# A gated MLP whose rows are normalised, scaled and split in row layout, and turned by DMA transposes instead of TensorE

## The reference

```python
h = shift_token(x)                       # columns 128..255 come from the row before
mu = h.mean(-1, keepdims=True)
var = h.var(-1, keepdims=True)
h = (h - mu) / jnp.sqrt(var + 1e-05) * lg + lb
h = h @ w1 + b1                          # 256 x 1364
a, g = jnp.split(h, 2, axis=-1)          # HID = 682 each
h = a * jax.nn.gelu(g, approximate=False)
x = x + h @ w2 + b2                      # 682 x 256
```

## Time and profile before

| | |
|---|---|
| median of three runs | 4297.88 us |
| profiled execution, its own time | 4296.06 us |
| its span | 4294.4 us |
| granted TensorE clock, mean over the span | 0.951 |
| busy over the span: TensorE, VectorE, ScalarE, GpSimd | 3835.2, 3330.0, 2558.9, 1191.1 us |

### The profile page before, as it was taken

One profiled execution on the slowest core, in us unless ns is written; L12 is line 12 of the kernel. 1 busy time (PEld: TensorE's weight loads), 2 busy tenths in 40 slices (PEclk: granted clock), 3 DMA queues, 4 the chain that ended last, 5 costly groups with the idle time before them and its releaser, 6 DMA issues. The chain is left out here.

```text
span 4294.4 us, 94790 instructions
## 1 busy us (share of the span) xinstructions
PE 3835.2 (89%) x38292; PEld 2167.2 (50%) x38292; DVE 3330.0 (78%) x5467; ACT 2558.9 (60%) x3449; POOL 1191.1 (28%) x966
## 2 busy tenths in 40 slices
PE   7999999769998969998986999999999999866996
PEld 4788888535655535555553332332333333334664
DVE  5688988779985569985687889999998978584444
ACT  3566666646553435653443777787888887744553
POOL 1022321267761067771141000000000000033552
PEclk9999999889999989999997999999999999977998
DMA  1010100133330033430072000000000000034664
GB/s 63 5 40 28 43 25 25 41 70 64 63 51 28 0 63 66 65 55 9 0 160 47 9 9 2 9 2 2 9 2 2 9 2 9 4 100 93 117 134 111
DMA packets 325878, 175.39 MB, mean 41 GB/s; under 512 B 239508, under 2 KB 316520, under 8 KB 324968
## 3 DMA queue, kind: packets, MB, share of 16 engines
q1 hardware_dynamic: 302856, 133.88, 14.8%
q0 software_dynamic: 13440, 21.24, 2.9%
q10 hardware_dynamic: 9184, 14.68, 1.4%
HBM read 77.81 MB, written 38.58 MB: 27 GB/s over the span
## 5 line engine op out<-in xcount | busy, mean ns | idle before, releaser
L2257 DVE TENSOR_REDUCE s_tops<-ps 128x2 f32<-128x1024 f32 (+3 forms) x1152 | 1252.2, 1132 | 143.2 <-PE ps L2143 103.6
L2226 ACT ACTIVATE s_weights<-ps 128x1024 f32<-128x1024 f32 (+3 forms) x1152 | 1092.5, 952 | 344.3 <-PE ps L2156 193.8
L2178 PE MATMUL ps<-s_weights,v_flat 128*32 128x256 f32 (+1 forms) x8704 | 692.1, 390 | 7.4 <-ACT s_o_t L2232 6.1
L2137 PE MATMUL ps<-keys,s_q 48*128 48x512 f16 (+3 forms) x2304 | 435.0, 375 | 46.0 <-DVE s_tops L2257 26.0
L2156 PE MATMUL ps<-s_q,keys 50*128 50x512 f16 (+3 forms) x2304 | 434.0, 374 | 46.9 <-DVE s_tops L2257 33.3
L2293 POOL CAST s_shift<-s_minus_top 128x16 f16<-128x16 f32 x32 | 6.3, 196 | 1429.9 <-DVE s_minus_top L2264 1429.9
L583 PE MATMUL ps<-a_qt,a_kt 128*128 128x256 f16 x3072 | 375.3, 273 | 3.8 <-POOL s_ones L538 3.8
L2156 PEld LDWEIGHTS ps<-s_q,keys 50*128 50x128 f16 x2304 | 112.2, 93 | 512.3 <-issue 246.7
L1174 PE MATMUL ps<-attention_w,la_yt 128*128 128x512 f16 x1152 | 289.3, 399 | 37.8 <-DMA la_yt<-la_y_parts 30.3
L583 PEld LDWEIGHTS ps<-a_qt,a_kt 128*128 128x128 f16 x3072 | 300.9, 98 | 40.3 <-POOL s_ones L538 4.2
L1249 ACT ACTIVATE la_weights<-ps 128x1024 f32<-128x1024 f32 x124 | 126.8, 1023 | 291.5 <-PE ps L1164 291.5
(11 more groups left out here) (372 smaller groups left out, 7158.0 us busy)
## 6 DMA issues: line engine op xcount, KB each, us to landing
ex_whole<-in_L_ffn_w_dram ACTq DMA_DIRECT2D x14, 1024.0 KB, 10.2
qk_parts<-a_parts SPq DMA_DIRECT2D x64, 128.0 KB, 4.3
keys<-qk_parts SPq DMA_DIRECT2D x48, 128.0 KB, 5.7
s_q<-qk_parts SPq DMA_DIRECT2D x48, 128.0 KB, 5.0
x<-in_x_dram SPq DMA_DIRECT2D x8, 512.0 KB, 9.3
attention_w<-attention_split SPq DMA_DIRECT2D x2, 2048.0 KB, 9.1
la_table<-in_rotary_dram SPq DMA_DIRECT2D x64, 64.0 KB, 2.1
a_table<-in_rope_dram POOLq DMA_DIRECT2D x8, 512.0 KB, 6.1
```

The source lines that it names most:

```text
L2137: mm = pe.matmul(m.ps[:, bank, 0:width], b.q[rows(half, KEY_PARTS * L1_DH), place % 2, pair, t * P:(t + 1) * P], m.keys[rows(half, KEY_PAR ...
L2178: mm = pe.matmul(m.ps[h * QUAD:(h + 1) * QUAD, OUT, begin:end], m.v_flat[:, first:first + QUAD], weights[:, a % 2, h, begin:end], start=(k ...
L2226: act.activation(weights[:, a % 2, 2 * pair:2 * pair + 2, skip:CHUNK], m.ps[:, bank:end + 1, skip:CHUNK], ACT.Exp).then_inc(s["exp"], 1)
L2257: dve.tensor_reduce(tops[:, u % 2, :, i % 2, t, c], m.ps[:, bank:end + 1, 0:width], AX.X, ALU.max).then_inc(s["max"], 1)
```

## The change

The rows stay in row layout until they are split. `norm` is as before, one count for each tile of rows. GpSimd multiplies by `ln_g` and adds `ln_b` (`gain`), which now have to be there as rows spread over all partitions, and two DMAs load them so. ScalarE rounds a chunk's high part (`high`), VectorE makes the low part (`parts_low`), and SP issues four DMA transposes that write `ht`. The shift by one row is not copied any more, apart from one column that GpSimd copies at a chunk's edge (`edge`): for the second half of the columns TensorE reads `ht` one column early (`EDGE - k`). PSUM banks 0 and 1 are free, and "up" has three pairs (`RING`) instead of two; two tiles of the next chunk (`AHEAD`) stand before down instead of one. Chunk 0 is made tile by tile by VectorE and ScalarE.

```diff
-    TURN_AT = ET - 4
-    NORMED_BY = {1: 0, 2: 1, 4: 2, 5: 3}
+    RING, AHEAD = 3, 2
+    EDGE = 16
+    HIGH_AT, LOW_AT = 0, 1
+    NORMED_BY = {0: 0, 1: 1, 2: 2, 3: 3}
...
-        ht_whole = sb("ht_whole", [P, 2, KD, CHUNK + 4])
-        ht = sb("ht", [P, 2, 2, KD, CHUNK], F16)
+        parts = sb("parts", [P, 2, TPC, 2, D], F16)
+        ht = sb("ht", [P, 2, 2, KD, EDGE + CHUNK], F16)
+        before = sb("before", [P, 1])
+        lng_row, lnb_row = sb("lng_row", [P, D]), sb("lnb_row", [P, D])
...
+                for to, name in ((lng_row, "ln_g"), (lnb_row, "ln_b")):
+                    sp.dma_start(to[:, :], layer_of(a[name], layer).rearrange("o d -> (o d)").partition_broadcast(P)).then_inc(s["rows_in"], 16)
...
+                def turn(c):
+                    if c:
+                        need(sp, s["low"], c)
+                        need(sp, s["ht"], 16 * TPC * c)
+                        need(sp, s["a_mm"], ET * (c - 1))
+                    for j in range(TPC):
+                        at = EDGE + j * P
+                        if c == 0:
+                            sp.wait_ge(s["first_low"], j + 1)
+                        sp.dma_start_transpose(ht[:, c % 2, :, :, at:at + P].rearrange("p a k t -> p (a k) t"),
+                                               parts[:, c % 2, j, :, :].rearrange("p a d -> p (a d)")).then_inc(s["ht"], 16)
+                turn(0)
                 move_down(sp, m, s, 1)
                 if not last:
                     load_attention(sp, m, a, layer + 1, s["next_in"])
                 move_up(sp, m, s, 1)
+                for c in range(1, CHUNKS):
+                    turn(c)
...
+                def edge(c, u):
+                    need(pool, s["ht"], 16 * TPC * (c + 1))
+                    need(pool, s["a_mm"], ET * c)
+                    pool.tensor_copy(ht[:, 1 - u, :, 1, EDGE - 1:EDGE], ht[:, u, :, 1, EDGE + CHUNK - 1:EDGE + CHUNK]).then_inc(s["edge"], 1)
+
+                def gain(c, u):
+                    for j in range(TPC):
+                        whole = normed[:, u, j, :]
+                        need(pool, s["normed"], TPC * (c - 1) + j + 1)
+                        pool.tensor_tensor(whole, whole, lng_row[:, :], ALU.mult).then_inc(s["gained"], 1)
+                        pool.wait_ge(s["gained"], TPC * (c - 1) + j + 1)
+                        pool.tensor_tensor(whole, whole, lnb_row[:, :], ALU.add).then_inc(s["whole"], 1)
+
+                def step(c, u):
+                    bias(c, u)
+                    if exists(c + 1):
+                        edge(c, u)
+                    if exists(c + 2):
+                        gain(c + 2, u)
+
+                pool.wait_ge(s["rows_in"], 32)
+                gain(1, 1)
                 rows_on_gpsimd(pool, m, s, 1)
-                in_pairs(pool, CHUNKS, bias)
+                for c in range(CHUNKS):
+                    step(c, c % 2)
...
-                    need(dve, s["turned"], KD * (c - 1))
+                    need(dve, s["low"], c - 2)
...
-                def ht_low(c, u):
-                    need(dve, s["a_mm"], ET * (c - 1))
-                    for k in range(KD):
-                        need(dve, s["ht_high"], KD * c + k + 1)
-                        dve.tensor_tensor(ht[:, u, 1, k, :], ht_whole[:, u, k, 0:CHUNK], ht[:, u, 0, k, :], ALU.subtract).then_inc(s["ht"], 1)
+                def parts_low(c, u):
+                    need(dve, s["high"], c)
+                    dve.scalar_tensor_tensor(parts[:, u, :, 1, :], normed[:, u, :, :], 1.0, parts[:, u, :, 0, :], ALU.mult, ALU.subtract).then_inc(s["low"], 1)
+                def whole_of_first(j):
+                    parts_of_row = [(slice(0, P), m.own), (slice(P, D), m.next)]
+                    for h, by in parts_of_row:
+                        n = dve.scalar_tensor_tensor(normed[:, 0, j, h], m.y[:, j, h], by[:, 0, j:j + 1], lng_row[:, h], ALU.subtract, ALU.mult)
+                    n.then_inc(s["first_gained"], 1)
+                    dve.wait_ge(s["first_gained"], j + 1)
+                    for h, by in parts_of_row:
+                        n = dve.scalar_tensor_tensor(normed[:, 0, j, h], normed[:, 0, j, h], by[:, 1, j:j + 1], lnb_row[:, h], ALU.mult, ALU.add)
+                    n.then_inc(s["first_whole"], 1)
+
+                def low_of_first(j):
+                    dve.wait_ge(s["first_high"], j + 1)
+                    dve.scalar_tensor_tensor(parts[:, 0, j, 1, :], normed[:, 0, j, :], 1.0, parts[:, 0, j, 0, :], ALU.mult, ALU.subtract).then_inc(s["first_low"], 1)
...
                 def gate(c, u, between=None):
-                    if exists(c + 2):
-                        dve.wait_ge(s["back"], 32)
...
-                        if e == TURN_AT + 1 and exists(c + 1):
-                            ht_low(c + 1, 1 - u)
-                        elif e and e <= TPC + 1 and exists(c + 2):
+                        if e == LOW_AT and exists(c + 1):
+                            parts_low(c + 1, 1 - u)
+                        if e in NORMED_BY and exists(c + 2):
                             norm(c + 2, u, range(NORMED_BY[e], NORMED_BY[e] + 1))
...
                     low(ET - 1)
+                    if exists(c + 2):
+                        dve.wait_ge(s["back"], 32)
...
-                norm(0, 0)
+                dve.wait_ge(s["rows_in"], 32)
+                for j in range(TPC):
+                    whole_of_first(j)
+                    if j:
+                        low_of_first(j - 1)
+                low_of_first(TPC - 1)
                 half_rows_on_vector(dve, m, s, 1)
+                dve.wait_ge(s["edge_high"], 1)
+                dve.tensor_tensor(ht[:, 0, 1, 1, EDGE - 1:EDGE], before[:, :], ht[:, 0, 0, 1, EDGE - 1:EDGE], ALU.subtract).then_inc(s["edge_low"], 1)
                 norm(1, 1)
-                ht_low(0, 0)
                 rows_on_vector(dve, m, s, 1)
                 dve.wait_ge(s["zeroed"], 1)
...
-                def scaled(c, u):
-                    need(act, s["ht"], KD * (c - 1))
-                    need(act, s["turned"], KD * c + 1)
-                    act.activation(ht_whole[:, u, 0, 0:CHUNK], m.ps[:, 0, :], ACT.Identity, bias=b.lnb[:, 0:1], scale=b.lng[:, 0:1]).then_inc(s["ht_whole"], 1)
-                    need(act, s["turned"], KD * c + 2)
-                    need(act, s["ht_whole"], KD * c)
-                    act.copy(ht_whole[:, u, 1, 0:1], ht_whole[:, 1 - u, 1, CHUNK:CHUNK + 1])
-                    act.activation(ht_whole[:, u, 1, 1:CHUNK + 1], m.ps[:, 1, :], ACT.Identity, bias=b.lnb[:, 1:2], scale=b.lng[:, 1:2]).then_inc(s["ht_whole"], 1)
-                    need(act, s["a_mm"], ET * (c - 1))
-                    for k in range(KD):
-                        need(act, s["ht_whole"], KD * c + k + 1)
-                        act.copy(ht[:, u, 0, k, :], ht_whole[:, u, k, 0:CHUNK]).then_inc(s["ht_high"], 1)
+                act.copy(ht[:, 0, 0, 1, EDGE - 1:EDGE], before[:, :]).then_inc(s["edge_high"], 1)
+
+                def high_of_first(j):
+                    act.wait_ge(s["first_whole"], j + 1)
+                    act.copy(parts[:, 0, j, 0, :], normed[:, 0, j, :]).then_inc(s["first_high"], 1)
+
+                def high(c, u):
+                    act.wait_ge(s["whole"], TPC * c)
+                    need(act, s["ht"], 16 * TPC * (c - 1))
+                    act.copy(parts[:, u, :, 0, :], normed[:, u, :, :]).then_inc(s["high"], 1)
...
-                            high(e - 1)
-                        if e == TURN_AT and exists(c + 1):
-                            scaled(c + 1, 1 - u)
-                    high(ET - 1)
-
-                scaled(0, 0)
+                            hid_high(e - 1)
+                        if e == HIGH_AT and exists(c + 1):
+                            high(c + 1, 1 - u)
+                    hid_high(ET - 1)
+
+                for j in range(TPC):
+                    high_of_first(j)
                 act.wait_ge(s["zeroed"], 1)
                 run(gelus, act.Fori)
...
-                def turn(c, u):
-                    need(pe, s["normed"], c + 1)
-                    for k in range(KD):
-                        need(pe, s["ht_whole"], KD * (c - 1) + k + 1)
-                        for j in range(TPC):
-                            t = pe.transpose(m.ps[:, k, j * P:(j + 1) * P], normed[:, u, j, k * P:(k + 1) * P], m.ident[:, :])
-                        t.then_inc(s["turned"], 1)
...
-                    need(pe, s["ht"], KD * (c + 1))
+                    need(pe, s["ht"], 16 * TPC * (c + 1))
+                    if isinstance(c, int) and c == 0:
+                        pe.wait_ge(s["edge_low"], 1)
+                    else:
+                        need(pe, s["edge"], c)
...
                         for part, mm_sem, free in ((1, s["g_mm"], s["gelu"]), (0, s["a_mm"], s["hid_whole"])):
-                            need(pe, free, ET * c + e - 2 + 1)
+                            need(pe, free, ET * c + e - RING + 1)
```

(42 more changed lines are left out.)

16 lines of the change are left out of this document (8 added, 8 removed).

## The result

The changed kernel takes 4317.02 us (median of 6 runs, 4310.10 to 4331.99), beside 4296.26 for the kernel before in the same rounds: a ratio of 1.005, interval 1.0039 to 1.0062; the medians lie 20.8 us apart. The forecast was 4311. The profiled execution took 4312.28, 16.2 more than that of before (4296.06), which is the comparison that the traces explain.

The account below looks back on a forecast made before the run. TensorE was taken as the bound, busy 114.66 of 118.2 us. Steady part +3.5, start +5, output stage -1.5 and clock +6 sum to +13; added to the median 4297.88 this gives 4311 us, range 4279 to 4333.

Parts of the forecast that it names:

- The saving, 1.95 a chunk: TensorE's steady MLP chunk: turn and wait for the last hid go, leaving 21.79 us if nothing else is late.
- What is late next: Tiles ahead wait 2.1 us for parts_low and four transposes after down; period 23.9 against 23.74, steady part +3.5.
- The collisions: GpSimd's gain beside VectorE's low(0) and parts_low at a chunk's start: 0 to 1.3 us, taken as 0.4.
- The start: Start of each MLP: first up 4.9 us later at 1316.6, first down's end +2.4 a layer, +5 for both.
- turn(1) not late: MLP start: the +5 leaves out a late turn(1), which appears only in the upper bound of +12.
- The end of a stage, no term: Each MLP's end unchanged: a 2.99 us wait for hid, then down takes 10.48 instead of 7.43.
- The output stage, -1.5: Output stage: take_h ahead of high cuts TensorE's wait by up to 1.04 at about two places; -1.5.
- The clock, +6 for 2 of 12: Two of twelve stalls at the tiles ahead drop TensorE's clock, 3.05 us for a slow down: +6, possible 0 to 37.
- D: Rival: up's reads shifted one element run at half pace, adding about 115 us: 4413; chance 0.03.
- C: Rival: transposes overlap, all four land by D + 9.1 (D: down's end), TensorE never stalls: period 21.79, 4278; chance 0.22.
- E: Rival: every stall at the tiles ahead costs clock, +37 in place of +6: 4342; chance 0.05.
- rival B: An even exchange: stalls cost no clock and collisions cancel, +2: 4300; chance 0.29.

Follow-up runs that it names:

- low_in_down: The changed kernel with parts_low(c+2) at the start of residual(c), beside down(c), a whole down earlier: 4294.99 us, ratio 0.9993.
- all_three: low_in_down with the rows of gain and shift loaded in the stage before and GpSimd's bias behind down's third tile: 4282.39 us, ratio 0.9960.
- swap_alone: The kernel before with only the output stage's swap, ScalarE's take_h ahead of high: 4299.00 us, ratio 1.0004.
- ahead_1: all_three with one tile of the next chunk ahead of down instead of two, three buffers kept: 4292.22 us, ratio 0.9986.
- one_piece: The changed kernel, but chunk 0's four transposes all wait until the last piece's low part is made: 4329.23 us, ratio 1.0072.
- low_at_2: The changed kernel with parts_low one tile later in gate, behind low(1): 4375.69 us, ratio 1.0178.

## Why the prediction was right, point by point

- **The saving, 1.95 a chunk: right.** 21.79 was forecast for a chunk with nothing late; low_in_down and all_three have 21.92, a saving of 1.82.
- **What is late next: right, in place and size.** L1554 started 3.08 behind down's end (3.00), the first tile ahead at 11.41 (11.3), the wait was 2.05 (2.1), the chunk 24.03 (23.9). From the first down's end to the seventh's layer 1 grew by 1.0 us (forecast 1) and layer 0 by 5.5, 1.7 of it clock (2.5 and clock): layer 0's waits were 2.3 to 2.8. One bound was summed wrongly: with the first tile ahead at 12.9 a chunk is 25.5 us, not 25.0, and the upper bound of the steady part +21, not +15.
- **The collisions: named, and undersized.** 0.64 instead of 0.4. Missed was the one that matters once the stall is gone: `bias`, in the new order behind `gain`, now starts just ahead of the gate's last two subtractions and stretches them from 1.46 to 3.44 or 5.54. And a `norm` (one tensor operand from SBUF) was not priced: it takes 0.75 beside `gain` instead of 0.34.
- **The start: the first up right (1316.27, forecast 1316.6), what follows undersized.** +2.4 a layer was forecast; less the tile more that is done by then (2.59), the first down ended 3.4 us later in layer 0 and 6.0 in layer 1. "turn(1) not late" failed: waits of 1.12 and 1.45. And the comparison was read from layer 0 alone, whose first chunk took 29.05 us from first matmul to down's end; layer 1's took 27.83. The same two chunks took 30.21 and 28.18 in swap_alone, so 1.5 of the 9.4 for both layers is within what an unchanged MLP differs by.
- **The end of a stage, no term: wrong for layer 1, and luck for layer 0.** Layer 0 got 2.9 us back because the clock stayed up, but so it did in swap_alone with the MLP of before; the prediction took the 10.48 of one execution for fixed. Layer 1 gave back 2.3 of the 2.59 that it should have saved, 1.1 of it wait: with a tile more done beforehand, VectorE's last gate with `add_to_x` has less under it, and the wait is 4.09 (4.49 in all_three, and 2.99 in ahead_1, which has one tile ahead). The other 1.2 is clock.
- **The output stage, -1.5: not borne out.** The wait moved to VectorE.
- **The clock, +6 for 2 of 12: too high in this execution, and priced too high.** One wait (2.31) was followed by slow matmuls, and they cost 1.7, not 3.05. In one_piece three of eleven such waits were, so the share of 2 in 12 is not refuted. That after's runs lie up to 19.7 above the profiled one could be more such drops; no trace of a slower run was taken, so it stays open.
- **The rivals.** D fell: the mean of the "up" matmuls is 380 ns with the shifted reads and 379 before. C is what happens once `parts_low` starts a chunk's down earlier; as the code stands it failed where the prediction said, at four landings by D + 9.1. E came true only for the longer waits of low_at_2.

Of the sum of +13, the MLPs had 14.5: steady part 3.5, start 5, clock 6. Measured were 15.0: about 4.8, 9.4 and 1.7, with -0.9 at the ends. So the mechanism (one longer wait, on the chain from down's end to the fourth transpose, for the turn and the old wait) was right, but that the total came so close is luck: two terms are wrong by 4 us each way, and layer 0's end gave 2.9 by its clock. The medians lie 6 us further up than this sum, and the range was wide enough to hold rival B too, so the rows and not the total show that the prediction was right.

## What to carry to other kernels

Work taken off the bounding engine is worth what the new chain's latency leaves: add up from the event that starts it (here the end of down, since VectorE's order put `parts_low` behind it) to the moment its result is wanted, and then ask which earlier place in the same engine's order has all its inputs ready. When an elementwise step moves to GpSimd, look at what stands behind it in GpSimd's order, not only at what it runs beside: here that was `bias`. And price a stage's start: two rows loaded one stage earlier gave 6.7 us, as much as the saving of 1.95 in more than three chunks. Last, before a difference is put down to a change, look for the same code in another trace: it showed here that 2.9 us at a layer's end come and go by themselves.
